# GpSimd takes over the row normalisation of six of ten chunks between two passes of a graph network

## Chip, cores and metric

The kernel runs on one core of a Trainium2 chip. The metric is the device time of one execution in microseconds (us); less is better. Engines are called as in the profile: PE is TensorE's matmul side, PEld its weight loads, DVE is VectorE, ACT is ScalarE, POOL is GpSimd, SP is SyncE.

## The reference

Four graph layers, each inside a residual and a layer normalisation, on 6250 nodes of 128 features and 106250 edges sorted by destination:

```python
x = layernorm(x + L0(x, ...))   # edge MLP, mean over the edges of a node, node MLP
x = layernorm(x + L1(x, ...))   # gcn + residual branch, then batch norm over the nodes
x = layernorm(x + L2(x, ...))   # mean of the neighbours, matmul, elu
x = layernorm(x + L3(x, ...))   # two relational convolutions (4 relations)

def layernorm(x): m = mean(x, -1); v = var(x, -1); return (x - m) / sqrt(v + 1e-5)
```

The change lies at the end of the second line: the rows of `x + L1(x)` are normalised, and L2 then sums them over the edges.

## The kernel before

The nodes are padded to 50 tiles of 128 rows, held in SBUF as `X` (128 x 50 x 128, f32), and handled in `CHUNKS` = 10 chunks of `CT` = 5 tiles. Five passes go over the edges. Passes 1 and 2 (`wide_*`) work in 13 steps (`WIDE`) of 16 groups of 512 edges. Twelve groups of a step are dense: PE multiplies `X`, split into a rounded high part `piece_hi` and a remainder `piece_lo`, with matrices of small edge counts, which lie in DRAM as uint8 (`adj`) and are loaded by SP (`a_load`, four slots of two chunks' counts each) and converted to f32 half on ACT (`counts_on_act`, L1303) and half on DVE (`counts_on_dve`, L1308). One chunk of one step is ten matmuls (L1358, five tiles by two pieces). The other four groups are sparse: GpSimd gathers rows of a DRAM table by indirect DMA (`fetch`, L642), and PE multiplies them with one-hot matrices (`segment`, L1344).

Each engine runs its own program in its own order; semaphores join them. Between passes 1 and 2 stands `batch_norm_*`: ACT scales, PE transposes back, DVE adds into `X` and takes the statistics of each row; then eight small DVE operations (`m_step` 1 to 8) make mean, reciprocal deviation and shift of all rows. What follows is the part that the change touches:

- Rows: `apply(k)` normalises the five tiles of chunk k, three on DVE (L2193, counted by `m_row`), two on ACT (L2244, counted by `m_row2`).
- Splits: `pieces_high(k)` on ACT (L1707) waits for both counts of chunk k, `pieces_low(k)` on DVE (L1711) for `x_high`. PE's `dense` of the first step of the pass waits for `x_low` of the chunk and for both halves of the counts; the conversion of chunk n waits until PE has used chunk n - 2 (`a_used`), since there are two count buffers.
- Order: chunks 0 to 3 are interleaved by hand in `batch_norm_dve` and `batch_norm_act`, up to the counts of chunk 3. Then both engines apply the rows of chunks 4 to 9 in one go, and only then enter `wide_dve` and `wide_act`, which split chunk 4, convert its counts, and so on to chunk 9. After the counts of chunk 5 ACT loads the table for the exponential (shown at L2409).
- SP (`batch_norm_sp`) stores chunk after chunk of `X` into the table of pass 2 (`table_mean`, L2278) once both counts of the chunk are there. Then `wide_sp` goes on to the loads of `adj` that are left (L1743). The first eight chunks' counts of the step are in SBUF already; those of chunks 8 and 9 come with the first of these loads.
- GpSimd clears `acc` (L700) when ACT has read it, and then waits in `slow_pool` until all ten stores have landed before it gathers.

Of the kernel before, what the change touches and what calls it, by code (L numbers as in the profile page):

```python
# [49 lines left out]
CT = 5  # L50
CH = CT * P
CHUNKS = -(-N // (2 * CH)) * 2
# [63 lines left out]
ALU = mybir.AluOpType  # L116
# [4 lines left out]
def gnn(nc, x_rows, x_cols, src, dst, first, etype, eweight, ea_cols, W1a, b1a, b2b, biases, weights, out):  # L121
    with ExitStack() as ctx:
        def sb(name, shape, dt=F32):
            return ctx.enter_context(nc.sbuf_tensor(name, shape, dt))

        def sem(name):
            return ctx.enter_context(nc.semaphore(name))
# [18 lines left out]
        acc = sb("acc", [P, 3, ACC])  # L146
# [30 lines left out]
        def weight(at, parts, n):  # L177
# [26 lines left out]
        row_mean, row_half, row_var, row_std, row_rstd, row_shift = (  # L204
            sb(f"row_{x}", [P, NT]) for x in ("mean", "half", "var", "std", "rstd", "shift"))
# [123 lines left out]
        gate = sem("gate")  # L329
# [4 lines left out]
        slow0_pre, slow0_sum, slow0_relu = sem("slow0_pre"), sem("slow0_sum"), sem("slow0_relu")  # L334
        slow_hot, slow_seg, slow_added = sem("slow_hot"), sem("slow_seg"), sem("slow_added")
        setup_step, setup_wide = sem("setup_step"), sem("setup_wide")
        pass_done, acc_zero, cleared = sem("pass_done"), sem("acc_zero"), sem("cleared")

        table_stored = [sems(f"table{p}_stored", (4, 2, 1, 2, 1)[p]) for p in range(5)]
        STORED = [None, (16 * CHUNKS // 2,) * 2, (16 * CHUNKS,), (16 * (BLKS - 2), 32), (16 * BLKS,)]  # L340
# [331 lines left out]
        def padded(g):  # L672
            return PADDED if g == GROUPS - 1 else 0
# [22 lines left out]
        def wide_pool(pool, p, before):  # L696
            if p == 2:
                pool.wait_ge(m_u, CHUNKS)
                pool.sem_inc(gate, 1)
                pool.memset(acc[:, 0, :], 0.0).then_inc(acc_zero, 1)  # L700
            slow_pool(pool, p, before)
            for it in range(WIDE):
                step = (p - 1) * WIDE + it
                for j in range(S):
                    if step:
                        pool.wait_ge(wide_seg, (step - 1) * S + j + 1)
                        pool.sem_inc(gate, 1)
                    fetch(pool, p, it * BODY + SPARSE[j], gat[j], wide_gathered[j], padded(it * BODY + SPARSE[j]))
# [66 lines left out]
        def by_tile(x):  # L775
            return x.rearrange("p (u w) -> p u w", u=U)
# [365 lines left out]
        def slow_dve(dve, p, before):  # L1142
            lead = LAG if p < 3 else 0
            if p >= 3:
                dve.memset(stat[:, WOFF:WOFF + 1], 0.0).then_inc(setup_step, 1)
            hots = hot_w if p < 3 else hot
            if p < 3:
                dve.wait_ge(acc_zero, p)
            else:
                dve.wait_ge(cleared, (p - 2) * BLKS)  # L1150

            def step(it, n):
                at = load_bases(dve, it * SLOTS + lead)
                for q in range(SLOTS + LAG):
                    if q < SLOTS:
                        to = hots[:, q % HOTS, :]
                        dve.wait_ge(slow_seg, n + (q + 1 + RING - HOTS))
                        g = it * SLOTS + q
                        (weighted_hot_of(dve, g, to) if p >= 3 else one_hot_of(dve, g, by_tile(to))).then_inc(slow_hot, 1)
                    if q >= LAG:  # L1160
                        there = acc[:, 0, bass.ds(at[q - LAG], WIN)]
                        dve.wait_ge(slow_seg, n + (q - LAG + 1 + RING))
                        dve.wait_ge(slow_added, n + (q - LAG + PRIME_BANK))
                        dve.tensor_tensor(there, there, bank[4 + q % 2][:, 0:WIN], ALU.add).then_inc(slow_added, 1)

            with dve.If(before > 0):
                if p < 3:
                    dve.memset(stat[:, WOFF:WOFF + 1], 0.0).then_inc(setup_wide, 1)
                with dve.Fori(0, before) as r:
                    round_setup(dve, p, r, lead, before + 1)  # L1170
                    with dve.Fori(0, ITERS) as it:
                        step(it, (before * (p - 1) + r) * GROUPS + it * SLOTS)
                if p < 3:
                    round_setup(dve, p, before, lead, before + 1)
            if p >= 3:
                round_setup(dve, p, before, 0, before + 1, True)
            dve.wait_ge(slow_added, before * (p * GROUPS) + PRIME_BANK)
            dve.wait_ge(slow_seg, before * (p * GROUPS) + RING)
            dve.sem_inc(gate, 1)
# [517 lines left out]
        def x_row(t):  # L1697
            return X[:, bass.ds(t, 1), :].rearrange("p o f -> p (o f)")
# [70 lines left out]
        def node0_pool(pool):  # L1769
            pool.wait_ge(n0_agg, BLKS)  # L1770
            pool.sem_inc(gate, 1)
            pool.memset(acc[:, 0, :], 0.0).then_inc(acc_zero, 1)

            def store(k, s, last):
                pool.wait_ge(n0_rows, k + 1)
                pool.sem_inc(gate, 1)
                pool.dma_start(node_rows(tables[1], k), rows[k]).then_inc(table_stored[1][s], 16)
            chunks(pool, store)
# [331 lines left out]
        def node1_dve(dve, it, j):  # L2110
# [23 lines left out]
        m_u, m_turn, m_sum, m_bn, m_step, m_root, m_row, m_row2 = (  # L2134
            sem(f"m_{x}") for x in ("u", "turn", "sum", "bn", "step", "root", "row", "row2"))

        def batch_norm_dve(dve):
# [22 lines left out]
            def body(k, s, last):  # L2160
                dve.wait_ge(m_turn, k + 1)
                for t0, n, b in TILES_BACK[s]:
                    x = X[:, bass.ds(k * CT + t0, n), :]
# [26 lines left out]
            def apply(k):  # L2190
                for t in range(ON_DVE):
                    t = k * CT + t
                    ins = dve.tensor_scalar(x_row(t), x_row(t), row_mean[:, bass.ds(t, 1)], row_rstd[:, bass.ds(t, 1)],  # L2193
                                            ALU.subtract, ALU.mult)
                ins.then_inc(m_row, 1)
# [8 lines left out]
            apply(3)  # L2204
            pieces_low(dve, 3)
            counts_on_dve(dve, WIDE * PARTS + 3)
            for k in range(4, CHUNKS):
                apply(k)

        def pieces_low(dve, k):  # L2210
            if k < CHUNKS:
# [2 lines left out]

        def pieces_high(act, k):
            if k < CHUNKS:
                act.wait_ge(m_row, k + 1)
                act.wait_ge(m_row2, k + 1)
                split_high(act, k, X[:, k * CT:(k + 1) * CT, :])

        M_VAR, M_SHIFT = 6, 8
        ON_DVE = 3
        TILES_BACK = (TILES_IN, ((0, 3, 0), (3, 2, 1)))

        def batch_norm_act(act):
            act.wait_ge(n1_one, 1)
            act.activation(stat[:, STDB:STDB + 1], mv_y[:, 1:2], ACT.Sqrt, bias=stat[:, EPSC:EPSC + 1]).then_inc(n1_one, 1)
            act.wait_ge(n1_one, 6)

            def body(k, s, last):  # L2230
                if later(k, 2):
                    act.wait_ge(m_turn, k - 1)
                    act.sem_inc(gate, 1)
                act.activation(b_bn[:, s, :], acc[:, 0, cols(k)], ACT.Identity, bias=stat[:, SHIFT:SHIFT + 1],
                               scale=stat[:, SCALE:SCALE + 1]).then_inc(m_u, 1)
            chunks(act, body)
            act.wait_ge(m_step, M_VAR)
            act.activation(row_std[:, :], row_var[:, :], ACT.Sqrt, bias=stat[:, EPSC:EPSC + 1], scale=1.0 / F).then_inc(m_root, 1)
            act.wait_ge(m_step, M_SHIFT)

            def apply(k):
                for t in range(ON_DVE, CT):
                    t = k * CT + t
                    ins = act.activation(x_row(t), x_row(t), ACT.Identity, bias=row_shift[:, bass.ds(t, 1)],  # L2244
                                         scale=row_rstd[:, bass.ds(t, 1)])
                ins.then_inc(m_row2, 1)

            apply(0)
            pieces_high(act, 0)
            apply(1)  # L2250
            pieces_high(act, 1)
            apply(2)
            pieces_high(act, 2)
            counts_on_act(act, WIDE * PARTS + 2)
            apply(3)
            pieces_high(act, 3)
            counts_on_act(act, WIDE * PARTS + 3)
            for k in range(4, CHUNKS):
                apply(k)

        def batch_norm_pe(pe):
            def body(k, s, last):
                pe.wait_ge(m_u, k + 1)
                if later(k, 2):
                    pe.wait_ge(m_sum, k * 2 - 2)
                for t0, n, b in TILES_BACK[s]:
                    for j in range(n):
# [3 lines left out]

        def batch_norm_sp(sp):
            def store(k, s, last):
                sp.wait_ge(m_row, k + 1)
                sp.sem_inc(gate, 1)
                sp.wait_ge(m_row2, k + 1)
                sp.sem_inc(gate, 1)
                sp.dma_start(node_rows(tables[2], k), X[:, bass.ds(k * CT, CT), :]).then_inc(table_stored[2][0], 16)  # L2278
            chunks(sp, store)

# [562 lines left out]
```

## Time and profile before

| | us |
|---|---|
| runs before: median of 3 (lowest, highest) | 3854.82 (3853.2, 3858.64) |
| span of the profiled execution (one core) | 3853.9 |
| busy in it: PE, DVE, ACT, POOL | 3543.0, 2277.3, 2073.2, 2650.7 |
| row normalisation begins, PE's pass 2 begins | 1582.85, 1585.64 |
| gathers of pass 2 begin, of pass 3 begin | 1604.64, 1993.85 |

The page gives no time for the profiled execution other than its span; the span lies 0.9 us below the median of the runs. All instants are counted from the start of the span. Instructions of one engine are pipelined, so that a duration can be longer than the distance to the next start. TensorE's granted clock is given as a share of 2.4 GHz: 0.50 is the level of 1.2 GHz, 1.00 that of 2.4 GHz.

### The profile page before, as it was taken

To read this page: it belongs to the slowest core of one execution; us is meant where nothing else is said; L and a number is where in the kernel's file an instruction comes from. 1 tells how busy PE (TensorE), PEld (TensorE's weight loads), DVE (VectorE), ACT (ScalarE), POOL (GpSimd) and SP (SyncE) were. 2 spreads that over 40 slices of the span, in tenths; PEclk is the share of its full clock that TensorE was granted. 3 is DMA by queue.
4 is the path that set the end of the run, shared out by engine and by line. 5 is a ranking of instruction groups with operands and counts; after the bars stand their busy time and mean duration, and the time that the engine had idled before them with its cause. 6 is when DMAs were issued, how large, how long until landed. Compare 5 with 4: busy or idle time off the path is not lost. (4 is left out here: it accounts for less than half of the span.)

```text
span 3853.9 us, 70135 instructions
## 1 busy us (share of the span) xinstructions
PE 3543.0 (92%) x23444; PEld 3114.9 (81%) x23444; DVE 2277.3 (59%) x7846; ACT 2073.2 (54%) x4844; POOL 2650.7 (69%) x2744
## 2 busy tenths in 40 slices
PE   7999999999999999799979998998996889998898
PEld 5998888888887999688857777777775888888897
DVE  6998998989876555666664454454441233333242
ACT  4555555555546555566665555555545445454443
POOL 5777777777752666355547777777776777777776
PEclk8999999999999999799988999999998899999898
DMA  7666666666675666466634454445453445455453
GB/s 234 191 190 189 183 189 186 186 188 190 183 214 132 159 165 161 114 160 167 161 112 159 160 172 168 163 167 173 158 172 116 141 160 178 151 168 170 150 170 119
DMA packets 438782, 642.44 MB, mean 167 GB/s; under 512 B 266434, under 2 KB 310978, under 8 KB 438275
## 3 DMA queue, kind: packets, MB, share of 16 engines
q1 hardware_dynamic: 310322, 375.66, 30.3%
q0 software_dynamic: 100880, 235.32, 22.7%
q10 hardware_dynamic: 27202, 26.78, 2.2%
q8 instruction: 194, 3.18, 0.3%
q14 instruction: 184, 1.51, 0.1%
HBM read 468.80 MB, written 168.73 MB: 165 GB/s over the span
## 5 line engine op out<-in xcount | busy, mean ns | idle before, releaser
L642 POOL DMA_INDIRECT work<-table_rel,reli x1462 | 1383.4, 946 | 493.4 <-issue 438.6
L642 POOL DMA_INDIRECT work<-table_pre,srci x831 | 821.9, 989 | 263.3 <-issue 260.0
L1604 PEld LDWEIGHTS bank<-work 128*128 128x128 f32 x2928 | 392.4, 213 | 217.7 <-DMA work<-table_rel,reli 211.2
L1604 PE MATMUL bank<-work 128*128 128x72 f32 x2928 | 403.9, 298 | 177.6 <-DMA work<-table_rel,reli 177.4
L2597 ACT ACTIVATE work<-iota,local 128x72 f32<-128x72 f32 x1464 | 377.9, 342 | 324.3 <-PE bank L1604 323.2
L2602 ACT ACTIVATE work<-work,ew,src_both 128x72 f32<-128x72 f32 x1464 | 514.9, 434 | 6.1
L1358 PE MATMUL bank<-counts,piece_hi 128*128 128x432 f32 x1300 | 482.6, 371 | 34.8 <-DVE counts L1308 22.8
L1358 PE MATMUL bank<-counts,piece_lo 128*128 128x432 f32 x1300 | 468.7, 361 | 0.0
L1020 ACT ACTIVATE X<-bank 128x468 uint8<-128x468 f32 (+1 forms) x624 | 328.0, 543 | 243.0 <-PE bank L962 239.0
L923 PE MATMUL bank<-w_both,work 128*128 128x256 f32 x1664 | 433.4, 386 | 16.4 <-DMA work<-ea_cols 8.6
L935 PE MATMUL bank<-work 128*128 128x64 f32 x3328 | 399.7, 274 | 8.1 <-DVE hist L804 7.2
L935 PEld LDWEIGHTS bank<-work 128*128 128x128 f32 x3328 | 394.3, 193 | 14.4 <-issue 11.3
L1027 ACT ACTIVATE work<-work 128x512 f32<-128x512 f32 x416 | 254.1, 629 | 213.2 <-DVE work L857 211.9
L1532 DVE COPY work<-bank 128x440 f32<-128x440 f32 x200 | 115.9, 614 | 365.4 <-PE bank L1640 359.2
L642 POOL DMA_INDIRECT work<-table_mean,srci x207 | 204.4, 988 | 179.9 <-PE bank L1344 99.2
L857 DVE TENSOR_TENSOR work<-work,bank 128x512 f32<-128x512 f32 x416 | 267.0, 682 | 102.3 <-DMA work<-table_pre,srci 97.3
L923 PEld LDWEIGHTS bank<-w_both,work 128*128 128x128 f32 x1664 | 290.2, 192 | 42.6 <-DMA work<-ea_cols 8.9
L1358 PEld LDWEIGHTS bank<-counts,piece_hi 128*128 128x128 f32 x1300 | 245.8, 189 | 56.6 <-issue 18.5
L642 POOL DMA_INDIRECT work<-table_gcn,srci x207 | 206.5, 998 | 115.6 <-issue 59.0
L962 PE MATMUL bank<-X 128*128 128x234 bf16 (+3 forms) x2080 | 261.3, 251 | 9.0 <-ACT X L1020 8.3
L1629 PE MATMUL bank<-work,late_lo 128*128 128x440 bf16 x1050 | 244.7, 369 | 14.2 <-DVE work L1507 12.7
L1358 PEld LDWEIGHTS bank<-counts,piece_lo 128*128 128x128 f32 x1300 | 246.1, 189 | 14.2 <-issue 2.4
(322 smaller groups left out, 6117.7 us busy)
## 6 DMA issues: line engine op xcount, KB each, us to landing
work<-ea_cols SPq DMA_DIRECT2D x208, 256.0 KB, 2.9
kept<-work SPq DMA_DIRECT2D x50, 880.0 KB
kept<-w_both SPq DMA_DIRECT2D x50, 880.0 KB
work<-kept SPq DMA_DIRECT2D x50, 880.0 KB
w_both<-kept SPq DMA_DIRECT2D x50, 880.0 KB
adj<-X SPq DMA_DIRECT2D x156, 225.0 KB
work<-adj SPq DMA_DIRECT2D x65, 540.0 KB
work<-table_rel,reli POOLq DMA_INDIRECT x1462
```

The costliest lines, as they stand in the source:

```text
L642: pool.indirect_dma_start(into[:, u, :], None, tables[p], bass.IndirectOffsetOnAxis(ap=idx_of(p)[:, t:t + 1].bitcast(U32), axis=0)).then_i ...
L857: dve.tensor_tensor(g, g, bank[q % 2 * 2 + h][:, :], ALU.add).then_inc(pre_added, 1)
L923: mm = pe.matmul(bank[q % 2 * 2 + h][:, j * HID:(j + 1) * HID], ea[:, slot, u * P:(u + 1) * P], w1a[:, 1, :], start=True, stop=True)
L935: pe.matmul(into[:, c * WIN:(c + 1) * WIN], gat0[:, q % SLOTS0, u, c * F:(c + 1) * F], hot0[:, hq, u, 0:WIN], start=(u == 0), stop=(u == U ...
L962: mm = pe.matmul(into[:, :, A_OFF[u]:A_OFF[u] + w], hot_lo[q % HOTS][:, u, :], code[:, j % A_CODES, at:at + (hi - lo) * w].rearrange("p (h ...
L1020: act.activation(stage[:, j % A_STAGES, lo * AW:hi * AW], bank[A_BANKS_AT[b % 2]][:, 0:(hi - lo) * AW], ACT.Copy).then_inc(a_taken, 1)
L1027: act.activation(pairs, pairs, ACT.Relu).then_inc(done, 1)
L1358: mm = pe.matmul(bank[D_BANKS[step % 2]][:, 0:D * AW], x[:, i * CT + t, :], counts[n % 2][:, t, :], start=(i == 0 and t == 0 and x is piec ...
L1604: mm = pe.matmul(bank[4 + m % LATE_BANKS][:, 0:PAIR_WIN], late_gat[n % LATE][:, u, :], late_hot[:, n % LATE_HOTS, u * PAIR_WIN:(u + 1) * P ...
L1629: mm = pe.matmul(bank[A_BANKS_AT[u % 2]][:, 0:RHI * CW], late_lo[:, n // RANGES % 2, u * PIECES + i, :], late_code[n % 2 * U + u], start=( ...
L2597: ins = act.activation(hot3[:, u, :], iota[:, 0:PAIR_WIN], ACT.Abs, bias=local[:, t:t + 1], scale=-1.0)
L2602: ins = act.activation(hot3[:, u, :], hot3[:, u, :], ACT.Relu, bias=ew[:, t:t + 1], scale=src_lo[:, t:t + 1])
```

## The change

Chunks 0 to 3 stay as they are. The rows of chunks 4 to 9 (30 tiles of 128 x 128) leave DVE (18 instructions) and ACT (12 instructions) and go to GpSimd, as 30 `tensor_scalar` instructions behind its clearing of `acc` and ahead of its gathers. They wait for `m_step` 8. One semaphore, `pool_made` (the former `acc_zero`), counts the clears and then the chunks. ACT's `pieces_high` and SP's stores wait for it from chunk 4 on. The order of everything else is the same.

```diff
@@ wide_pool, p == 2
-                pool.memset(acc[:, 0, :], 0.0).then_inc(acc_zero, 1)
+                pool.memset(acc[:, 0, :], 0.0).then_inc(pool_made, 1)
+                batch_norm_pool(pool)
             slow_pool(pool, p, before)
@@ batch_norm_dve
             counts_on_dve(dve, WIDE * PARTS + 3)
-            for k in range(4, CHUNKS):
-                apply(k)
@@ pieces_high
-                act.wait_ge(m_row, k + 1)
-                act.wait_ge(m_row2, k + 1)
+                if k < ROWS_SHARED:
+                    act.wait_ge(m_row, k + 1)
+                    act.wait_ge(m_row2, k + 1)
+                else:
+                    act.wait_ge(pool_made, ROWS_MADE + k - ROWS_SHARED + 1)
                 split_high(act, k, X[:, k * CT:(k + 1) * CT, :])
@@
+        ROWS_SHARED, ROWS_MADE = 4, 2
+
+        def batch_norm_pool(pool):
+            pool.wait_ge(m_step, M_SHIFT)
+            pool.sem_inc(gate, 1)
+            for k in range(ROWS_SHARED, CHUNKS):
+                for t in range(k * CT, (k + 1) * CT):
+                    ins = pool.tensor_scalar(x_row(t), x_row(t), row_mean[:, t:t + 1], row_rstd[:, t:t + 1],
+                                             ALU.subtract, ALU.mult)
+                ins.then_inc(pool_made, 1)
@@ batch_norm_act
             counts_on_act(act, WIDE * PARTS + 3)
-            for k in range(4, CHUNKS):
-                apply(k)
@@ batch_norm_sp, store
-                sp.wait_ge(m_row, k + 1)
-                sp.sem_inc(gate, 1)
-                sp.wait_ge(m_row2, k + 1)
-                sp.sem_inc(gate, 1)
+                if k < ROWS_SHARED:
+                    sp.wait_ge(m_row, k + 1)
+                    sp.sem_inc(gate, 1)
+                    sp.wait_ge(m_row2, k + 1)
+                    sp.sem_inc(gate, 1)
+                else:
+                    sp.wait_ge(pool_made, ROWS_MADE + k - ROWS_SHARED + 1)
+                    sp.sem_inc(gate, 1)
                 sp.dma_start(node_rows(tables[2], k), X[:, bass.ds(k * CT, CT), :]).then_inc(table_stored[2][0], 16)
```

## Rows read from the trace of the kernel before

**Rows 1.** The page: busy time, share of the span and instructions of each engine.

```profile
PE 3543.0 (92%) x23444; PEld 3114.9 (81%) x23444; DVE 2277.3 (59%) x7846; ACT 2073.2 (54%) x4844; POOL 2650.7 (69%) x2744
```

**Rows 2.** Busy time by stretch: length, then each engine, PE's granted clock, DMA share.

```profile
1660.00:1990.00 330.00, 305.99 (x1627) 265.87 (x1626) 202.56 (x590) 201.68 (x222) 164.66 (x167) 0.99 0.56 152
...
1596.30:1600.50 4.20, 0.07 (x1) 0.00 (x0) 3.79 (x12) 4.20 (x9) 0.00 (x0) 1.00 1.04 285
1600.50:1604.20 3.70, 3.64 (x11) 3.39 (x12) 1.74 (x3) 3.36 (x4) 0.00 (x0) 0.55 1.02 253
1604.20:1614.10 9.90, 9.90 (x52) 9.42 (x51) 7.60 (x13) 8.17 (x8) 7.33 (x8) 0.99 1.14 250
1614.10:1622.50 8.40, 7.03 (x40) 6.45 (x39) 5.39 (x16) 4.50 (x4) 6.57 (x7) 1.00 0.65 170
```

**Rows 3.** Timeline of PE: start, duration, instruction, idle time before and its releaser.

```profile
1585.64 0.70 PE L1358 MATMUL bank<-counts,piece_hi 128*128 128x432 f32 x1 [9.58 <-issue]
...
1596.02 0.36 PE L1358 MATMUL bank<-counts,piece_lo 128*128 128x432 f32 x1
1600.56 0.43 PE L1358 MATMUL bank<-counts,piece_hi 128*128 128x432 f32 x1 [4.19 <-DVE counts L1308]
...
1619.48 0.43 PE L1358 MATMUL bank<-counts,piece_hi 128*128 128x432 f32 x1 [1.37 <-ACT counts L1303]
...
1621.51 1.00 PE L1344 MATMUL bank<-work 128*128 128x64 f32 x8
```

**Rows 4.** Timeline of DVE, from the first normalised row to the counts of chunk 4.

```profile
1582.85 1.63 DVE L2193 TENSOR_SCALAR X<-X,row_mean,row_rstd 128x128 f32<-128x128 f32 x6
1584.60 0.83 DVE L1711 TENSOR_TENSOR piece_lo<-X,piece_hi 128x640 fp32r<-128x640 f32 x1
...
1593.94 4.69 DVE L2193 TENSOR_SCALAR X<-X,row_mean,row_rstd 128x128 f32<-128x128 f32 x18
1598.96 0.83 DVE L1711 TENSOR_TENSOR piece_lo<-X,piece_hi 128x640 fp32r<-128x640 f32 x1 [0.33 <-ACT piece_hi L1707]
1599.70 0.72 DVE L1308 CAST counts<-work 128x900 fp32r<-128x900 uint8 x1
```

**Rows 5.** Timeline of ACT over the same stretch, with the table load.

```profile
1593.58 4.72 ACT L2244 ACTIVATE X<-X,row_shift,row_rstd 128x128 f32<-128x128 f32 x12
1598.20 0.72 ACT L1707 ACTIVATE piece_hi<-X 128x640 fp32r<-128x640 f32 x1
1598.83 1.24 ACT L1303 ACTIVATE counts<-work 128x1260 fp32r<-128x1260 uint8 x1
...
1601.86 1.28 ACT L2409 ACT_TABLE_LOAD   x1
```

**Rows 6.** Timeline of SP's queue: the ten stores, then the first load of counts.

```profile
1583.87 16.12 SPq L2278 DMA_DIRECT2D table_mean<-X  x10
1600.18 0.98 SPq L1743 DMA_DIRECT2D work<-adj  x1
```

**Rows 7.** Line L2278, the stores of 320 KB: time from issue to landing.

```profile
DMA to landing us min/median/max: 2.5/3.5/4.7
```

**Rows 8.** Timeline of POOL: two operations of the set-up, two of the gathers.

```profile
11.68 0.19 POOL L494 MEMSET ident<- 128x128 f32 x1
...
13.69 0.28 POOL L507 TENSOR_SCALAR_AFFINE_SELECT ident<-ident 128x128 f32<-128x128 f32 x1
...
1604.64 0.95 POOL L642 DMA_INDIRECT work<-table_mean,srci  x1 [25.41 <-DMA table_mean<-X]
...
1608.61 1.32 POOL L642 DMA_INDIRECT work<-table_mean,srci  x1 [0.30 <-issue]
```

**Rows 9.** Line L1308, DVE's half of the counts: least, median, longest duration in ns.

```profile
L1308 DVE CAST counts<-work x130: 696/722/954, 1220.1 to 1953.6; 128x900 fp32r<-128x900 uint8 x130
```

**Rows 10.** Waits in pass 2, 1614 to 1990 us: total, times, longest.

```profile
POOL work L642 <- PE bank L1344: 99.2, 32, 4.0
```

**Rows 11.** Timeline at the start of pass 3: the first gather.

```profile
1993.85 0.95 POOL L642 DMA_INDIRECT work<-table_rel,reli  x1 [30.26 <-DMA table_rel<-work]
```

More of the change, by code:

```diff
@@ L336, in gnn @@
         setup_step, setup_wide = sem("setup_step"), sem("setup_wide")
-        pass_done, acc_zero, cleared = sem("pass_done"), sem("acc_zero"), sem("cleared")
+        pass_done, pool_made, cleared = sem("pass_done"), sem("pool_made"), sem("cleared")
         table_stored = [sems(f"table{p}_stored", (4, 2, 1, 2, 1)[p]) for p in range(5)]
@@ L1147, in slow_dve @@
             if p < 3:
-                dve.wait_ge(acc_zero, p)
+                dve.wait_ge(pool_made, p)
             else:
@@ L1771, in node0_pool @@
             pool.sem_inc(gate, 1)
-            pool.memset(acc[:, 0, :], 0.0).then_inc(acc_zero, 1)
+            pool.memset(acc[:, 0, :], 0.0).then_inc(pool_made, 1)
             def store(k, s, last):
```

## The prediction

> **What bounds the kernel now.** I read the page's busy times first: PE is busy for 92% of the span, and no other engine for over 70% [rows 1]. That is an average over stages, so I went to the stretches around the change. From 1660 to 1990 us, deep in pass 2, PE is busy for 306 of 330 us at nearly full clock, while DVE, ACT and POOL are busy for about half to two thirds [rows 2]; of the waits there, the gathers' wait for PE to free a buffer is 99.2 us in total [rows 10]. So in pass 2 PE sets the pace, GpSimd runs behind it, and what PE does later or earlier at the start of the pass should come out at its end, where pass 3 starts its gathers on the last store of the relation table [rows 11].
>
> Then PE's timeline at the start of pass 2 [rows 3]. Its first dense matmul starts at 1585.64, forty of them (chunks 0 to 3) are issued by 1596.02, and then PE stands still for 4.19 us until DVE has the counts of chunk 4. The reader sees why in the timelines of DVE and ACT: from 1593.94 and from 1593.58 both normalise the rows of chunks 4 to 9, 4.69 and 4.72 us in one go [rows 4, 5], and the split and the counts of chunk 4 are queued behind. The table of stretches shows the second half of the price: the stretch of the standstill has PE busy for 0.07 us, and in the next 3.70 us the granted clock is 0.55, near the level of 1.2 GHz, before it is back at 0.99 [rows 2].
>
> **The change, part by part.**
>
> *The standstill.* Without the rows, ACT's split of chunk 4 can start at 1593.58 instead of 1598.20 [rows 5]. From the start of that split to the end of DVE's counts it is 1600.42 - 1598.20 = 2.22 us (DVE's low piece starts 0.04 us after the split's end, its counts 0.74 us later, and they take 0.72) [rows 4, 5], and PE starts 0.14 us later [rows 3]: PE could start chunk 4 at 1595.94. It is done issuing chunk 3 at 1596.02, and the next matmul follows 0.20 us later (below), so chunk 4 starts at 1596.22 instead of 1600.56: 4.3 us. This needs the rows of chunk 4 by 1593.58, 10.7 us after their statistics; GpSimd has five tiles to do in that time.
>
> *The clock.* Chunk 4's ten matmuls fill the stretch from 1600.56 to 1604.2, 3.6 us; the fifty of chunks 5 to 9 fill 9.9 us, 0.20 each, 2.0 a chunk [rows 2, 3]. Without the standstill nothing makes the clock fall, and chunk 4 too should take 2.0: another 1.6 us.
>
> *What takes the place.* With PE at 2.0 us a chunk, ACT is tight. Split and counts of a chunk take it some 1.8 us, and the table load of 1.28 us [rows 5], which hid in the slow stretch, now comes in the middle. The counts of chunk 5 wait until PE has used chunk 3 (1596.2), end about 1597.5, the table load about 1598.8; split, low piece and counts of chunk 6 are ready 2.2 us later, at 1601.0, and PE, which would be free at 1600.2, starts at about 1601.1. That gives back 0.9. A pause of this size does not cost the clock: after the 1.37 us before 1619.48 it stays at 1.00 [rows 2, 3].
>
> *The rows on GpSimd.* No instruction of this kind is in the trace. Below, a 128 x 128 memset takes 0.19 us; the one operation that reads and writes such a tile takes 0.28; above, a gather instruction, a quite different thing, takes 0.95 [rows 8]. Two column operands have to be fetched as well; I take 0.40, nearer to the 0.28, and with some waiting behind DVE 0.50 as the pace. Thirty tiles from 1582.9 on then end at 1597.9 (between 1588.6 and 1611.4 by the ends). The Trainium skill (GPSIMD Engine Reference, section Performance versus the Vector engine) gives about 2.6 cycles an element at 1.2 GHz for two-input work; an estimate from that is 0.28 us for 128 elements without the dispatch, so that the sum would be the same.
>
> *DVE beside GpSimd.* GpSimd now works on SBUF while DVE does the rows of chunks 0 and 1 and the first low piece, seven instructions ahead of PE's start at 1585.64, and while it does low piece and counts of chunk 3, two more that PE waits for. The trace has a hint that the two hinder each other: a gather of 1.32 us beside the usual 0.95 falls on DVE's busy stretch [rows 8], and a cast of DVE takes up to 954 ns beside 722 [rows 9]. If each of the nine waited for a whole GpSimd instruction of 0.28 us, it would be 2.5 us; if none did, nothing. I take half, 1.3. In the Trainium skill (SBUF — State Buffer, section Who interferes with whom) the rule is harsher: GpSimd shares one port pair with DVE, a DVE instruction with two SBUF inputs or in a fast copy mode and a GpSimd instruction that reads SBUF exclude each other, and whoever comes second waits for the whole instruction. The two long durations agree with it in direction, and by it the sum would take the upper end, 2.5; a result of its own is the last but one rival.
>
> *SP's queue.* Stores 4 to 9 now wait for GpSimd, and the load with the counts of chunks 8 and 9 is queued behind them on SP; before it was issued at 1600.18, just behind the tenth store [rows 6]. It is issued about 0.5 us after the last tile. A store of 320 KB lands after 2.5 us at best [rows 7]; 540 KB, at the 285 GB/s of the busiest stretch [rows 2], take 0.8 more, so 3.3. PE wants chunk 8 at 1596.2 + 4 x 2.0 + 0.9 = 1605.1, and the conversion takes 1.24 [rows 5]: the load must be there by 1603.8, and GpSimd must be done by 1600.0, or 1601.3 if the hindrance has made PE later by its 1.3. At 0.50 a tile it is, by 2 to 3 us; this is hidden, and its cover is used up at 0.57 to 0.61 us a tile.
>
> *GpSimd's own queue.* The gathers stand behind the rows, but they also waited for the stores before. With the last tile at 1597.9 the last store has landed near 1601.9, before 1604.64 [rows 8]. PE wants the first segment at 1621.51 less the gain; four gathers and their landing take some 8 us. Hidden too.
>
> *The sum.* 4.3 + 1.6 - 0.9 - 1.3 = 3.7 us. Against the profiled execution 3853.9 - 3.7 = 3850.2; its span lies 0.9 us below the median, so 3851.1 for the runs. That is 0.1%, and about 0.2% (7.7 us) is what a measurement of this kernel can tell from no change: its three runs lie 5.4 us apart.
>
> **The rivals.**
>
> 1. *GpSimd is a little slow, and the loads behind the stores eat the gain.* Between 0.61 and 0.73 us a tile each microsecond of GpSimd is one of PE's, at chunk 8; at 0.73 (last tile at 1604.9) nothing is left: 3852 to 3854.8, in the middle 3853. For it: the cover is only 0.1 us a tile, and the price of a tile is not in the trace. Against: the nearest row is 0.28.
> 2. *The two engines exclude each other, and the kernel gets slower.* By strict exclusion up to chunk 8 DVE's twelve rows, nine low pieces and seven casts (12 x 0.27 + 9 x 0.74 + 7 x 0.72 = 15.0 us [rows 4]) and GpSimd's 30 x 0.40 = 12.0 us add up to 27.0 us, so that the last tile is done at 1609.9. The load lands 3.8 us later, its conversion ends at 1614.9, and PE starts chunk 8 there instead of 1610.2 (1604.2 and three chunks): 4.7 us slower, 3859.5. It decides from 0.73 us a tile on, and it can be measured from about 0.95. For it: the two long durations; DVE's own 15.0 us have to fit into some 21 us. Against: DVE waits for ACT and PE between its instructions, and those gaps are free for GpSimd.
> 3. *The gain is there at chunk 9 and gone later*, since something else, such as the first gathers or the loads of the next step, paces the pass: 3854.8. For it: the DMA engines are full from 1596 to 1614 [rows 2]. Against: PE does not wait for the first segment [rows 3], and POOL waits for PE afterwards [rows 10].
> 4. *No hindrance at all*: 5.0 us, 3849.8, or, if ACT also fits its table load in, 3848.9.
>
> **How the numbers follow.** Chances: 0.57 for the forecast, 0.16 for the first rival, 0.14 for the second, 0.07 for the third, 0.06 for the fourth. The predicted time is 3851.1. Below, the range takes in the fourth rival and some spread of the runs, 3848; above, it takes in the first and third and the lower part of the second, 3858; outside are the strongest exclusion (0.11) and a better case than any that I can work out (0.06). Faster by over 0.2% needs a gain of 7.7 us, more than the whole standstill with its clock, 5.9: 0.05, from the spread of the runs. Slower by over 0.2% needs about 0.95 us a tile: 0.10, most of the second rival. The rest, 0.85, is within 0.2%.
>
> **What the changed profile would show.** PE: no idle time of 4 us ahead of chunk 4, clock near 1.00 from about 1592 to 1614, a pause of about 1 us near chunk 6, the last matmul of chunk 9 near 1610.5 instead of 1614.1. POOL: thirty instructions between the clearing of `acc` and the gathers, spaced 0.4 to 0.6 us. DVE: rows of chunks 0 and 1 spaced wider than 0.27 us, and PE's first matmul between 1585.6 and 1587.7. SP: the first load of counts before 1600. Pass 3's first gather about 3.7 us earlier than 1993.85. The prediction is wrong if a tile costs GpSimd over 0.6 us, if PE waits at chunk 8 for its counts, or if PE's first matmul is over 2.5 us late.

## Result, and the profile after

The changed kernel takes 3871.3 us (median of 5 runs, 3869.06 to 3876.28) against 3854.82 us before (5 runs, 3852.85 to 3858.64): a ratio of 1.0040, 95% interval 1.0029 to 1.0051. It is 16.5 us slower. The forecast was 3851.1, with a range up to 3858.0.

The span of its profiled execution is 3867.8 us, 13.9 more than before. The stages ahead of the change differ between executions by some microseconds either way (here the row statistics are ready at 1579.55 us, before at 1582.81), so the stretch that the change can touch is read from the end of the statistics to the first gather of pass 3: 411.0 us before, 2007.96 - 1579.55 = 428.4 us after, 17.4 more. From there to the end it is 1860.0 us before and 1859.8 after. So everything was lost in this stretch.

GpSimd's timeline after the change; a line is the start, the duration, the instruction, and the idle time before with its releaser:

```profile
1570.48 5.49 POOL L700 MEMSET acc<- 128x6472 f32 x1 [26.79 <-ACT work L2247]
1586.74 29.17 POOL L2232 TENSOR_SCALAR X<-X,row_mean,row_rstd 128x128 f32<-128x128 f32 x30 [10.77 <-issue]
1619.84 1.19 POOL L642 DMA_INDIRECT work<-table_mean,srci  x1 [3.92 <-DMA table_mean<-X]
```

The same line of the code, all its entries, with least, median and longest duration in ns:

```profile
L2232 POOL TENSOR_SCALAR X<-X,row_mean,row_rstd x30: 786/789/1826, 1586.7 to 1615.1; 128x128 f32<-128x128 f32 x30
L2232 POOLq MODIFY_POOL_CONFIG  x2: 11/11/11, 1579.8 to 1579.8; - x2
```

The statistics are ready at 1579.55, but the first row starts at 1586.74, 7.2 us later, and two entries that the kernel before did not have at this place stand at 1579.8. Then a row takes 0.97 us on the mean (29.17 / 30), not 0.40 or 0.50, and the last one is done at 1615.91: 36.4 us behind the statistics, where I had reckoned with 15.

What PE makes of it is in its timeline from the start of pass 2. Only the starts of chunks after idle time and the first segment are shown:

```profile
1582.37 0.70 PE L1359 MATMUL bank<-counts,piece_hi 128*128 128x432 f32 x1 [9.58 <-issue]
...
1590.86 0.44 PE L1359 MATMUL bank<-counts,piece_hi 128*128 128x432 f32 x1 [0.65 <-DVE counts L1309]
1594.48 0.43 PE L1359 MATMUL bank<-counts,piece_hi 128*128 128x432 f32 x1 [1.41 <-DVE counts L1309]
1599.02 0.43 PE L1359 MATMUL bank<-counts,piece_hi 128*128 128x432 f32 x1 [2.34 <-DVE counts L1309]
1603.92 0.70 PE L1359 MATMUL bank<-counts,piece_hi 128*128 128x432 f32 x1 [1.56 <-DVE counts L1309]
1608.99 0.70 PE L1359 MATMUL bank<-counts,piece_hi 128*128 128x432 f32 x1 [1.13 <-DVE counts L1309]
1622.54 0.70 PE L1359 MATMUL bank<-counts,piece_hi 128*128 128x432 f32 x1 [9.61 <-ACT counts L1304]
...
1635.96 1.00 PE L1345 MATMUL bank<-work 128*128 128x64 f32 x8
```

Chunk 3 starts 11.3 us behind the statistics, as before. The one standstill of 4.19 us [rows 3] has become a wait at each of the chunks 4 to 8, and the last of them is 9.61 us. Chunk 4 is even 2.8 us earlier than before (14.9 us behind the statistics, before 17.8), but chunk 8 is 15.7 us later (43.0, before 27.3). The first segment starts 56.4 us behind the statistics, before 38.7. The wait at chunk 8 is the load behind the stores, as SP's queue and VectorE's and ScalarE's timelines show:

```profile
1580.61 35.76 SPq L2293 DMA_DIRECT2D table_mean<-X  x10
1616.55 0.38 SPq L1744 DMA_DIRECT2D work<-adj  x1
```

```profile
1621.18 0.72 DVE L1309 CAST counts<-work 128x900 fp32r<-128x900 uint8 x1 [8.17 <-DMA work<-adj]
```

```profile
1611.42 0.74 ACT L1708 ACTIVATE piece_hi<-X 128x640 fp32r<-128x640 f32 x1 [3.09 <-POOL X L2232]
1621.18 1.25 ACT L1304 ACTIVATE counts<-work 128x1260 fp32r<-128x1260 uint8 x1 [9.03 <-DMA work<-adj]
```

The ten stores now take 35.8 us of the queue, before 16.1 [rows 6]; the load of the counts of chunks 8 and 9 is issued 0.6 us behind the last row and lands by 1621.18, when both casts start: 5.3 us behind the last row, where I had reckoned with 3.8. And by stretch (length, busy time of PE, PEld, DVE, ACT, POOL, granted clock, DMA share), from the rows' end to the first matmul of chunk 8:

```profile
1616.00:1622.50 6.50, 0.00 (x0) 0.00 (x0) 1.05 (x2) 1.32 (x2) 2.36 (x2) 0.56 0.95 225
```

PE does nothing for 6.5 us, and the clock is at its lower level when it starts again. It had fallen before: over the stretch from 1600 to 1616 us the granted clock is 0.58, after PE's wait of 2.34 us ahead of chunk 5.

One of the runs below, of the early instruction behind the clearing, took 4724.43 us at a mean granted clock of 0.692 and stands in no figure here.

### The profile page after: what moved, and what is told of

Its sections match the earlier page's. It is cut to its first block and busy times, and to the rows that moved or that the text cites. A ratio compares the mean times of both kernels' runs of the same rounds, so it can differ in the third digit from the quotient of the medians.

```text
span 3867.8 us, 70126 instructions
## 1 busy us (share of the span) xinstructions
PE 3548.6 (92%) x23444; PEld 3122.3 (81%) x23444; DVE 2270.1 (59%) x7828; ACT 2066.8 (53%) x4832; POOL 2676.6 (69%) x2774
```

## Experiments

"Stretch" is the time from the statistics to the first gather of pass 3, from one profiled execution each. Ratios are to the kernel before on the same chip.

**The worth of the standstill.** The row instructions are left out:

```diff
-                for t in range(k * CT, (k + 1) * CT):
-                    ins = pool.tensor_scalar(x_row(t), x_row(t), row_mean[:, t:t + 1], ...)
-                ins.then_inc(pool_made, 1)
+                pool.memset(warm[:, k - ROWS_SHARED:k - ROWS_SHARED + 1], 0.0).then_inc(pool_made, 1)
```

> The change with the 30 row instructions left out: chunks 4 to 9 are not normalised, GpSimd signals them at once by six memsets of one column. This is the most that the change could have brought. My sum without hindrance (4.3 + 1.6 - 0.9 = 5.0 us): 3849.8. Theory B (the standstill of 4.2 us is made up for later in pass 2 in any case): 3854.8.

3851.07 us against 3856.51, ratio 0.9985 (0.9975 to 0.9995); the stretch is 405.7, 5.3 below before. PE's waits up to the first segment of this kernel:

```profile
1602.65 0.43 PE L1360 MATMUL bank<-counts,piece_hi 128*128 128x432 f32 x1 [1.13 <-DVE counts L1310]
1616.19 0.44 PE L1360 MATMUL bank<-counts,piece_hi 128*128 128x432 f32 x1 [1.26 <-DVE counts L1310]
```

The standstill is gone. What is left is a pause ahead of chunk 6, where I had put the one of ScalarE's table load, and one before the first segment that was there before [rows 3]. The terms come out one by one: chunk 4 starts 4.4 us nearer to the statistics than before (forecast 4.3), chunk 5, with the clock, 5.9 (5.9), chunk 6, with the pause, 4.7 (5.0). The gain of 5.0 was rightly sized and does carry through pass 2. So all of the 17.4, and these 5.3 on top, are the price of the rows on GpSimd: 22.7 us.

**The late start.** One GpSimd instruction of the same kind, on one column, early in its idle time:

```diff
             if p == 2:
+                pool.tensor_scalar(warm[:, 1:2], one[:, :], one[:, :], one[:, :], ALU.subtract, ALU.mult)
                 pool.wait_ge(m_u, CHUNKS)
...
```

> The change, with one more GpSimd tensor_scalar on a single column ahead of its wait for the end of pass 1, where it is idle. In the changed kernel GpSimd's first row starts 7.2 us after the statistics are ready, behind two MODIFY_POOL_CONFIG entries. Theory A (a one-time loading of code for this operation, which the early instruction takes on itself): the first row starts within 0.5 us of the eighth m_step, the last ends some 7 us earlier, the load of counts too, and the time falls by 5 to 7 us, to about 3865. Theory B (the delay comes whenever GpSimd turns from its clearing to this operation, or from its own queue): the gap stays near 7 us and the time near 3871. The rows then also run beside VectorE's rows of chunks 0 and 1, so that it is seen whether PE's first matmul comes later: by my sum up to 2 us, by theory C (VectorE is not held up, only GpSimd is) not at all.

The rows start at once, 0.2 us behind the statistics:

```profile
L699 POOLq MODIFY_POOL_CONFIG  x2: 37/37/37, 1549.8 to 1549.9; - x2
1557.11 0.74 POOL L699 TENSOR_SCALAR warm<-one 128x1 f32<-128x1 f32 x1 [7.35 <-issue]
1576.19 5.49 POOL L702 MEMSET acc<- 128x6472 f32 x1 [18.34 <-ACT work L2249]
1585.46 30.97 POOL L2234 TENSOR_SCALAR X<-X,row_mean,row_rstd 128x128 f32<-128x128 f32 x30 [3.78 <-DVE row_shift L2190]
```

The 7 us are now ahead of the early instruction, whose entries of MODIFY_POOL_CONFIG stand at 1549.8, and the clearing in between does not bring them back. Theory A holds: the delay comes once, with the first such instruction; that it is a loading of code, the trace does not show by itself. The thirty rows take 31.0 us here instead of 29.2, since more of them meet VectorE's low pieces, so that the last ends 5.2 us earlier and not 7. The stretch falls to 422.5, 5.9 below the change. But the time was 3885.01, ratio 1.0072 (1.0056 to 1.0089), since passes 3 and 4 took 1876.5 us instead of 1859.8; that is taken up below. The run also shows VectorE's six rows of chunks 0 and 1 while GpSimd does its own:

```profile
1585.29 1.63 DVE L2196 TENSOR_SCALAR X<-X,row_mean,row_rstd 128x128 f32<-128x128 f32 x6
```

They take 1.63 us as before [rows 4], and PE's first matmul (1588.07) comes 2.8 us behind the statistics (1585.25), as before. Theory C holds for these six rows and for PE's start.

**The same, behind the clearing** of `acc` instead of ahead of it.

> The change with the early one-column tensor_scalar right behind GpSimd's clearing of acc and ahead of its wait for the statistics, not ahead of the clearing. The early instruction ahead of the clearing took the loading away (first row 0.2 us behind the statistics), but the gathers of passes 3 and 4 then took 955 ns instead of 944 each, 16 us over 1462 of them. Theory A (the loading starts as soon as the queue reaches the instruction): the clearing ends 3.6 us ahead of the statistics, so the first row is about 3.5 us late instead of 7.2, and the time is 2 to 4 us below the change, about 3868, if the gathers stay at 944. Theory B (one more instruction of this kind makes the gathers slower wherever it stands): gathers near 955 and some 3880.

3881.64 us (median of three runs) against 3856.52, ratio 1.0074 (1.0056 to 1.0092). The first row starts 3.7 us behind the statistics, as the loading by theory A asks, and the stretch is 425.4, 3.0 below the change; the gathers of passes 3 and 4 again take 956 ns each on the mean, as theory B asks.

**The order on SP.** The first load of counts ahead of the store of chunk 4:

```diff
             def store(k, s, last):
+                if k == 4:
+                    sp.wait_ge(act_counts, 2 * WIDE * LOADS + 2)
+                    sp.sem_inc(gate, 1)
+                    sp.wait_ge(dve_counts, 2 * WIDE * LOADS + 2)
+                    sp.sem_inc(gate, 1)
+                    a_load(sp, WIDE * LOADS + A_SLOTS)
...
```

> The change, with the first load of counts (chunks 8 and 9) issued by SP ahead of the store of chunk 4 instead of behind the store of chunk 9. Theory A (the loads queued behind the stores hold PE at chunk 8): the wait of 9.6 us ahead of chunk 8 shrinks to the 1 to 3 us that the rows themselves cost, chunk 8 starts about 2.3 us after its rows, and the time falls by 5 to 7 us, to about 3865. Theory B (GpSimd's rows alone set the pace, the loads only come along): 3871, no change, with PE waiting for the split of chunk 8 instead.

3868.26 us, ratio 1.0029 (1.0017 to 1.0040); the stretch is 423.3, 5.1 below the change. By the runs alone the gain over the change (ratio 1.0040, 1.0029 to 1.0051) is not clear of noise, and theory A had asked for 3865. PE's starts of chunks 8 and 9, and of the first chunk of the second step:

```profile
1617.55 0.70 PE L1359 MATMUL bank<-counts,piece_hi 128*128 128x432 f32 x1 [1.75 <-DVE counts L1309]
1622.35 0.70 PE L1359 MATMUL bank<-counts,piece_hi 128*128 128x432 f32 x1 [0.86 <-DVE counts L1309]
1626.82 0.70 PE L1359 MATMUL bank<-counts,piece_hi 128*128 128x432 f32 x1 [0.53 <-ACT counts L1304]
```

The wait of 9.6 us is gone, and what is left is PE going from chunk to chunk at the pace of GpSimd's rows, near 5 us a chunk, at the lower clock for the last ones. The queue cost 5 us of the stretch; the other 12 are what the rows cost by themselves, late start and clock included.

**The price of a row, by width and operands.** Half the columns, then numbers in place of the two column operands:

```diff
-   pool.tensor_scalar(x_row(t), x_row(t), row_mean[:, t:t + 1], row_rstd[:, t:t + 1], ...)
+   pool.tensor_scalar(x_row(t)[:, 0:F // 2], x_row(t)[:, 0:F // 2], row_mean[:, t:t + 1], row_rstd[:, t:t + 1], ...)
```

```diff
-   pool.tensor_scalar(x_row(t), x_row(t), row_mean[:, t:t + 1], row_rstd[:, t:t + 1], ...)
+   pool.tensor_scalar(x_row(t), x_row(t), 0.0, 1.0, ALU.subtract, ALU.mult)
```

> The change with GpSimd normalising only 64 of the 128 columns of each row in chunks 4 to 9 (the others are left as they were). In the changed kernel the undisturbed distance from row to row is 0.78 us. Theory A (the price is by the element, 6 ns each): 0.4 us. Theory B (most of it is fixed, for the instruction and its two column operands): 0.65 us or more.

> The change with GpSimd's 30 instructions taking the numbers 0 and 1 in place of the two column operands, so that chunks 4 to 9 are not normalised; tile, width and the two operations stay. With 128 columns the undisturbed distance was 0.78 us, with 64 columns it was some 0.57, so about 0.36 fixed and 3.3 ns a column. Theory A (the fixed part is the fetch of the column operands): 0.5 us or less. Theory B (the price lies in the operation itself): 0.7 us or more. The start, 7 us behind the statistics, should stay by either.

The row instructions of the first, then of the second (least, median, longest in ns):

```profile
L2232 POOL TENSOR_SCALAR X<-X,row_mean,row_rstd x30: 571/576/1633, 1593.1 to 1614.1; 128x64 f32<-128x64 f32 x30
```

```profile
L2232 POOL TENSOR_SCALAR X<-X x30: 637/642/1463, 1587.2 to 1608.7; 128x128 f32<-128x128 f32 x30
```

Against 789 ns: 64 columns fewer save 213 ns, 3.3 ns a column, so by a line through the two widths 0.36 us are there without any column; the column operands make up 0.15 us of the 0.79. No theory of either pair was right: about half is by the column, a fifth is the operands. The stretches are 421.3 and 422.3, and one run each took 3869.15 and 3864.67 us.

**GpSimd beside VectorE.** VectorE's low pieces of chunks 4 to 9 as a clearing:

```diff
-                split_low(dve, k, X[:, k * CT:(k + 1) * CT, :])
+                if k < ROWS_SHARED:
+                    split_low(dve, k, X[:, k * CT:(k + 1) * CT, :])
+                else:
+                    dve.memset(piece_lo[:, k * CT:(k + 1) * CT, :].bitcast(F32), 0.0).then_inc(x_low, 1)
```

> The change with VectorE's low pieces of chunks 4 to 9 replaced by a clearing, which reads nothing (the low part of those rows is left out of the sums). In the changed kernel each of six GpSimd rows that meets a low piece and the cast behind it takes 1.45 to 1.83 us instead of 0.79, 5.9 us in all. Theory A (GpSimd's read and a VectorE instruction with two SBUF inputs exclude each other, and GpSimd waits): the long rows shrink to what the cast alone costs, 1.2 us or less, and the thirty rows end 2 to 5 us earlier. Theory B (it is the cast, or something other than VectorE): they stay at 1.5 us or more.

```profile
L2235 POOL TENSOR_SCALAR X<-X,row_mean,row_rstd x30: 783/788/1367, 1588.4 to 1612.6; 128x128 f32<-128x128 f32 x30
```

The longest row is 1.37 us instead of 1.83; it stands at chunk 3, whose low piece and cast are as before. Beside the casts of chunks 4 to 7 four rows take 1.07 us each. The thirty take 25.0 us instead of 29.2; undisturbed, at a distance of 0.775, they would take 23.3. So of the 5.9 us lost to VectorE the low pieces of chunks 4 to 9 make up 4.2; of the 1.7 that are left, four casts make up 1.1 and chunk 3 the rest. Theory A holds as far as the low pieces are the cause; whether the two exclude each other or only slow each other down, this run does not tell. The median is the same: the rows that meet neither are not touched. The stretch is 425.2, and the one run took 3866.88 us.

**Versions made from this.** GpSimd only for chunks 7 to 9; VectorE and ScalarE do the others one chunk ahead, and SP's first load comes first:

```diff
             if k < CHUNKS:                     # pieces_low, the same on ScalarE
                 dve.wait_ge(x_high, CHUNKS + k + 1)
                 split_low(dve, k, X[:, k * CT:(k + 1) * CT, :])
+                if 3 <= k < ROWS_SHARED - 1:
+                    rows_dve(dve, k + 1)
...
-        ROWS_SHARED, ROWS_MADE = 4, 2
+        ROWS_SHARED, ROWS_MADE = 7, 2
```

> A version made from the findings: GpSimd takes only chunks 7 to 9 (15 rows), VectorE and ScalarE do chunks 4 to 6, one chunk ahead of each split instead of all in one go, and SP issues the first load of counts ahead of the store of chunk 4. Theory A (what made the change slow is that GpSimd's rows and the loads behind them come later than PE wants them): GpSimd is done with chunk 7 some 12 us, chunk 8 some 17 us and chunk 9 some 22 us behind the statistics, PE wants them at about 20, 22 and 24, so PE has no wait over 2 us, and the time is 2 to 4 us below the kernel before, about 3853 beside 3856. Theory B (the new work on ScalarE, 2.6 us a chunk beside PE's 2.0, and the rows of GpSimd cost as much as the standstill): no change, 3856.

3853.31 us against 3856.52, ratio 0.9992 (0.9983 to 1.0001): 3.2 us less, as theory A asks, but not clear of noise. The stretch of the profiled execution, the longest of its eleven runs (3858.43 us), is 412.0, not below the 411.0 of before. The late start is still there (first row 7.2 us behind the statistics), the 15 rows took 17.8 us, 1.2 each, with more of them beside VectorE's work, and the last ended 25.0 us behind the statistics and not 22. PE waited up to 1.2 us at a chunk of the first step, and 2.2 us at the first of the second. Between the two theories this run does not decide. The same without GpSimd (`ROWS_SHARED` 10 and no rows on it):

> Without GpSimd: VectorE and ScalarE do the rows of all of chunks 4 to 9, one chunk ahead of each split instead of all in one go, and SP issues the first load of counts ahead of the store of chunk 4; GpSimd does no rows. Theory A (GpSimd's three chunks were what kept the version with chunks 7 to 9 on it at the level of the kernel before): the stretch from the statistics to the first gather of pass 3, 411.0 us before and 412.0 with three chunks on GpSimd, falls to 408 or 409, and the time to some 2 or 3 us below the kernel before. Theory B (ScalarE, with rows, split and counts of 2.6 us a chunk beside PE's 2.0, is what holds PE as soon as the standstill is gone): 410 to 411, no measurable change.

3852.99 us against 3852.94, ratio 0.9998 (0.9989 to 1.0007), stretch 412.3. Theory B holds here: with VectorE and ScalarE doing more in between, PE waits at each of the chunks 3 to 8 and again at the start of the second step (0.3 to 1.8 us each), and these waits come to about what the one standstill cost. No version beat the kernel before by more than the measurement can tell.

**The slower gathers** of the two kernels with an early instruction:

```diff
 # the kernel before, with one early instruction
+                pool.tensor_scalar(warm[:, 1:2], one[:, :], one[:, :], one[:, :], ALU.subtract, ALU.mult)
 # the change, with the last row in two halves: 31 instructions
+                    for c in ((0, F),) if t < NT - 1 else ((0, F // 2), (F // 2, F)):
```

> The kernel before with one single-column tensor_scalar more on GpSimd, in its idle stretch ahead of the clearing of acc, and nothing else. Both runs with such an early instruction had gathers of 955 ns instead of 944 in passes 3 and 4. Theory A (the one-column instruction, or the loading of its code at that place, leaves GpSimd slower at gathers): 955 ns, and some 16 us more than the kernel before, 3872. Theory B (it needs the 30 rows behind it): 944 ns and the time of before, 3856.

> The change with the last row in two instructions of 64 columns, so 31 of them instead of 30 and no early one. Theory A (the one-column instruction is what makes the gathers slower): gathers stay at 944 ns and the time near that of the change. Theory B (it is the number of instructions that GpSimd's program holds ahead of the gathers): 955 ns and some 16 us more.

3849.94 us against 3852.94, ratio 0.9990 (0.9980 to 0.9999), and 3867.3 us; gathers of 946 ns on the mean in both. So neither the early instruction by itself nor the number 31 makes gathers slower: theory B of the first and theory A of the second hold as far as the gathers go, and what is slower in the two kernels with both is not explained.

## Why the prediction was wrong

The step that failed is the time at which GpSimd's rows are done: 15.0 us behind the statistics in the sum, 36.4 in the trace (7.2 of late start, 23.3 for the tiles, 5.9 of waiting beside VectorE). All that the sum had as hidden behind it was then on PE's path.

*What the change takes away* was right in mechanism and size: 5.0 reckoned, 5.3 to 5.4 measured, with a pause where that of the table load was forecast.

*The rows on GpSimd* is the term that was mis-sized. I bounded the tile by a memset and a gather, took 0.40 us, near the affine select of the set-up [rows 8], and 0.50 with waiting. A tile costs 0.78 undisturbed. The select has no column operands, but these explain only 0.15 of the difference; that an operation on the same tile costs GpSimd 0.28 says little about another one. Against 30 x 0.50 = 15.0 us this term came out at 23.3, plus 5.9 of waiting, 29.2 together; even the upper end, thirty tiles at 0.95, was 28.5. The estimate of 0.28 us for 128 elements without the dispatch does not agree with the runs either: 128 columns at 3.3 ns are 0.43, and 0.36 stand beside them.

*A start of 7.2 us* was not in the sum at all; the sum put it at nothing, without a reason. The trace of before has the hint, in the set-up, on a line that I had not read: GpSimd's reduction over partitions has the same two entries, and runs only 7.7 us behind them (VectorE, which it waits for too, may be part of that).

```profile
L516 POOLq MODIFY_POOL_CONFIG  x2: 16/16/16, 27.8 to 27.8; - x2
L516 POOL PARTITION_ALL_REDUCE stat<-stat x1: 380/380/380, 35.5 to 35.5; - x1
```

The Trainium skill (GPSIMD Engine Reference, section Instruction dispatch) tells of a load of about 6 us, measured as 5.95, between MODIFY_POOL_CONFIG and the first instruction of a newly loaded kernel; here it is 6.9 us from 1579.8 to 1586.74, and the run with the early instruction shows that it comes once. I had not brought it to bear, because I took the operation for one that is always at hand. Whether the code for the rows was in place during the set-up, beside the affine select, and was displaced by that reduction, was not tried.

*DVE beside GpSimd* had the victim wrong in the main. I charged VectorE, and so PE, 1.3 us; PE's first matmul and its chunk 3 came as far behind the statistics as before (2.8 and 11.3 us), and GpSimd lost 5.9. Single instructions of VectorE did take longer: a low piece 0.93 and a cast 0.89 us in the changed kernel, and in the run without low pieces that of chunk 3, which stays, 1.12 us, beside a row that kept its 0.79. The rule of the Trainium skill (SBUF — State Buffer, section Who interferes with whom) agrees with these records as far as a low piece and a row hinder each other, and the run without low pieces agrees; that whoever comes second waits, most of them do not bear out. Of the changed kernel, a row on GpSimd, and then the two instructions of VectorE that it meets:

```profile
1592.64 1.65 POOL L2232 TENSOR_SCALAR X<-X,row_mean,row_rstd 128x128 f32<-128x128 f32 x1
```

```profile
1592.69 0.93 DVE L1712 TENSOR_TENSOR piece_lo<-X,piece_hi 128x640 fp32r<-128x640 f32 x1 [1.98 <-ACT piece_hi L1708]
1593.54 0.80 DVE L1309 CAST counts<-work 128x900 fp32r<-128x900 uint8 x1
```

The row had started 0.05 us before the low piece, and it is the one that took twice its time. Five of the six long rows meet a low piece and a cast; the last one meets a low piece alone, and 0.66 us of its 1.45 are lost to it:

```profile
1612.15 1.45 POOL L2232 TENSOR_SCALAR X<-X,row_mean,row_rstd 128x128 f32<-128x128 f32 x1
```

```profile
1612.18 0.82 DVE L1712 TENSOR_TENSOR piece_lo<-X,piece_hi 128x640 fp32r<-128x640 f32 x1 [3.02 <-ACT piece_hi L1708]
```

*SP's queue* had the place right: the load queued behind the stores made PE wait at chunk 8, as it was to do past 0.57 to 0.61 us a tile. That figure itself was not tried, since the tiles came out far beyond it: counted from the statistics, 36.4 us for 30 tiles is 1.21 a tile. The landing was put 1.5 us too short (3.8 reckoned, 5.3 measured). The second rival named the place too, and 0.73 us a tile as the point of no gain. Its arithmetic (14.4 us past that point) gives 3869, near the 3871 measured, and the landing and the lower clock of chunk 8, which takes 3.7 us instead of 2.0, can make up the rest. The reason that it gave, strict exclusion at 0.40 a tile, would have come to 4.7 us, a third of that. I gave it 0.14.

*Passes 3 and 4*, which the sum left as they were, took the same: 1860.0 us before, 1859.8 after.

## What to carry to other kernels

An operation that an engine has not run yet in this program has no price in the profile: measure it by itself, in the place where it is to stand, before it is put on a path with a cover of 0.1 us a tile. Work that a slower engine takes over delays not only its readers but whatever is queued behind its stores; here a load that PE needed stood behind them, and to move it was worth 5 us. And what stops an engine once for 4 us was not won here by spreading the same work over the engines that feed it: without GpSimd chunk followed chunk after some 2.5 us, and PE needs 2.0 for one. A version that joins an early instruction with a small share for GpSimd was not tried.

## What the runs showed of the hardware

- GpSimd's first `tensor_scalar` came 6.9 us behind two MODIFY_POOL_CONFIG entries; the clearing and the gathers around it had none. With an early one (7.3 us behind its entries) the rows behind the clearing had no such entries and started 0.2 us behind the statistics.
- A `tensor_scalar` of 128 x 128 f32 with two column operands took GpSimd 0.79 us, with 64 columns 0.57; a line through the two leaves 0.36 with no column at all.
- GpSimd's rows that met a low piece and a cast of VectorE took up to 1.83 us, one that met a low piece alone 1.45, four beside a cast alone 1.07 in the run without low pieces; VectorE's own low pieces and casts in the changed kernel took 0.82 to 0.93 and 0.71 to 0.89 us then.
- In both kernels with an early one-column instruction and thirty rows the gathers took 11 ns longer (median 955 instead of 944), from pass 2 to the end. The lines are of the run with the early instruction ahead of the clearing; the second is of pass 1, ahead of both:

```profile
L643 POOL DMA_INDIRECT work<-table_rel,reli x1462: 951/955/1450, 2007.8 to 3870.1; - x183
L643 POOL DMA_INDIRECT work<-table_gcn,srci x207: 940/947/1257, 1231.8 to 1548.8; - x104
```

1462 times 11 ns is 16 us, about what passes 3 and 4 lost (16.7 and 15.5 us in the two). The early instruction alone does not do it, nor do 31 instructions; why the two together do stays open.
